# A DLRM tower on one core: the reshaping of the field rows issued from ScalarE, layer 1's items placed later in a step

## What is computed

```python
e = jnp.stack([tbl_f[ids[:, f]] for f in range(24)], axis=1)    # (1024, 24, 16)
X0, Xk, outs = e, e, []
for W in (W0, W1, W2):                                          # 64 outputs each
    Wr = W.reshape(24, Xk.shape[1], 64)
    Xk = jnp.einsum('bfd,bhd,fho->bod', X0, Xk, Wr)
    outs.append(Xk.sum(axis=2))
z = jnp.concatenate(outs, axis=1)
h = jnp.concatenate([z, dense_ctx], axis=1)
h = jnp.maximum(h @ W_top1 + b_top1, 0.0)
h = jnp.maximum(h @ W_top2 + b_top2, 0.0)
y = h @ W_top3
```

## Time and profile before

| | |
|---|---|
| median of 3 runs | 455.85 us (454.94 to 456.58) |
| the profiled execution | 455.96 us, its span 454.1 us |
| TensorE busy | 373.9 us (82%) |
| VectorE busy | 303.0 us (67%) |
| ScalarE busy | 127.6 us (28%) |
| GpSimd busy | 196.5 us (43%) |
| DMA | 64.76 MB, 143 GB/s in the mean |
| mean granted TensorE clock | 0.962 |

### The profile page before, as it was taken

One profiled execution on the slowest core, in us unless ns is written; L12 is line 12 of the kernel. 1 busy time (PEld: TensorE's weight loads), 2 busy tenths in 40 slices (PEclk: granted clock), 3 DMA queues, 4 the chain that ended last, 5 costly groups with the idle time before them and its releaser, 6 DMA issues. The chain is left out here.

```text
span 454.1 us, 6457 instructions
## 1 busy us (share of the span) xinstructions
PE 373.9 (82%) x2436; PEld 140.1 (31%) x2436; DVE 303.0 (67%) x305; ACT 127.6 (28%) x228; POOL 196.5 (43%) x196
## 2 busy tenths in 40 slices
PE   0005957995699899889998998899899998999997
PEld 0002201221134134312441243234333421443554
DVE  1003439887657995899599949994999498991000
ACT  1003000331222333234233333233414241127433
POOL 5777777787777877877707760000000000000000
PEclk9999975996889999999999999999989999999999
DMA  7000088366776787678766776876587558700000
GB/s 205 7 7 7 8 203 199 89 180 173 177 169 184 194 199 172 175 196 201 182 183 184 190 184 193 204 186 190 157 204 190 160 154 208 187 2 0 1 0 0
DMA packets 27203, 64.76 MB, mean 143 GB/s; under 512 B 7247, under 2 KB 10759, under 8 KB 27180
## 3 DMA queue, kind: packets, MB, share of 16 engines
q1 hardware_dynamic: 21036, 62.87, 51.4%
q0 software_dynamic: 6144, 1.59, 3.8%
HBM read 58.06 MB, written 6.38 MB: 142 GB/s over the span
## 5 line engine op out<-in xcount | busy, mean ns | idle before, releaser
L395 DVE TENSOR_TENSOR pairs<-spread,units 128x1024 f32<-128x1024 f32 x192 | 223.3, 1220 | 20.3 <-DMA units<-x_dram 13.1
L367 POOL DMA_INDIRECT emb<-in_tbl,ids_sb x192 | 196.3, 1023 | 74.2 <-issue 57.6
L593 PE MATMUL acc<-pairs,w_sb 128*64 128x512 f32 x768 | 200.3, 624 | 15.7 <-DVE pairs L395 14.6
L395 DVE TENSOR_TENSOR pairs<-turned,common 120x1024 f32<-120x1024 f32 x42 | 51.2, 1220 | 40.9 <-DMA turned<-x_dram 34.4
L593 PEld LDWEIGHTS acc<-pairs,w_sb 128*64 128x64 f32 x768 | 45.4, 139 | 106.9 <-DVE pairs L395 52.9
L593 PE MATMUL acc<-pairs,w 120*64 120x512 f32 x180 | 52.3, 666 | 9.9 <-DVE z L400 5.9
L567 PE MATMUL spread<-x0parts,sel 72*128 72x512 bf16 (+1 forms) x140 | 47.2, 426 | 11.2 <-DVE pairs L395 9.1
L455 ACT ACTIVATE x<-acc 128x512 f32<-128x512 f32 x31 | 18.6, 599 | 117.4 <-PE acc L593 117.4
L610 PE MATMUL misc<-ident_b,parts 128*72 128x128 bf16 x120 | 10.4, 235 | 39.9 <-DVE parts L297 37.0
L468 ACT ACTIVATE x0diag<-misc,mask 128x384 f32<-128x384 f32 x64 | 31.7, 611 | 15.2 <-PE misc L613 15.2
L628 PEld LDWEIGHTS misc<-x0diag,x2t 128*64 128x64 f32 x512 | 26.0, 137 | 18.8 <-issue 16.5
(11 more groups left out here) (38 smaller groups left out, 143.5 us busy)
## 6 DMA issues: line engine op xcount, KB each, us to landing
units<-x_dram SPq DMA_DIRECT2D x64, 512.0 KB, 7.5
turned<-x_dram SPq DMA_DIRECT2D x42, 480.0 KB
x_dram<-x SPq DMA_DIRECT2D x32, 128.0 KB
emb<-in_tbl,ids_sb POOLq DMA_INDIRECT x192
x_dram<-common SPq DMA_DIRECT2D x14, 96.0 KB
x_dram<-common SPq DMA_DIRECT2D x14, 56.0 KB
w_sb<-in_w SPq DMA_DIRECT2D x2, 384.0 KB
wt_sb<-in_wt SPq DMA_DIRECT2D x1, 512.0 KB, 5.5
```

Of the source, the lines that this page charges most:

```text
L367: pool.indirect_dma_start(out=e3[:, f, :], out_offset=None, in_=tables[f], in_offset=bass.IndirectOffsetOnAxis(ap=ids_sb[:, t, f:f + 1], a ...
L395: dve.tensor_tensor(pairs[buf][0:rows, :], source[0:rows, :], other[0:rows, h * HALF:(h + 1) * HALF], ALU.mult).then_inc(pairs_done, 1)
L593: last = pe.matmul(acc[half * H:(half + 1) * H, :], w, pairs[buf][0:rows, half * BLK:(half + 1) * BLK], start=first, stop=final)
```

## The change

ScalarE now issues the stores of common's rows and the loads of turned. `store_fields` follows each `take_common` at once. The three loads for h = 0 are issued at places 7, 8 and 8 of ScalarE's loop (three and four behind the first common), those for h = 1 two places behind the L1 item of h = 0 that frees the buffer. SyncE keeps only the reshaping of x1. In the middle steps and in step 6 the L1 items move from places 12, 14, 16, 21, 23, 26 to 14, 16, 18, 22, 24, 26; step 0 keeps its places. The copy of x1's first half moves with its last item from place 19 to 21.

```diff
+L1_AT = (14, 16, 18, 22, 24, 26)
-MIDDLE = Plan((12, 14, 16, 21, 23, 26), (4, 8), (0, 1), SIDE, {20: 2})
+MIDDLE = Plan(L1_AT, (4, 8), (0, 1), SIDE, {20: 2})
...
-BEFORE_LAST = Plan((12, 14, 16, 21, 23, 26), (4, 8), (0, 1), SIDE)
+BEFORE_LAST = Plan(L1_AT, (4, 8), (0, 1), SIDE)
...
             for t in range(1, TILES):
-                for h in range(2):
-                    turn_fields(t, h)
                 for h in range(2):
                     spread_units(t, t % 2, h)
...
+            def store_fields(i, h):
+
+                act.wait_ge(common_done, 2 * (i + 1) + h + 1)
+                for first, rows in ((0, F), (F, X0_ROWS - F)):
+                    act.dma_start(x0_dram[h][first:first + rows, :],
+                                  common[0:rows * J_CHUNK:J_CHUNK, h * HALF:(h + 1) * HALF]).then_inc(x0_stored[h], 16)
+
+            def turn_fields(i, h, c):
+
+                if c == 0:
+                    act.wait_ge(x0_stored[h], 32 * (i + 1))
+
+                if h == 1:
+                    act.wait_ge(pairs_done, item(i, plan(i).items.index(("L1", c, 0, 0))) + 1)
+                elif has_last(i):
+                    act.wait_ge(pairs_done, item(i - 1, MIDDLE.items.index(("L1", c, 0, 1))) + 1)
+                rows = x0_dram[h][c * J_CHUNK:c * J_CHUNK + F, :].rearrange("f (j x) -> f j x", j=1)
+                strides = [list(d) for d in rows.ap]
+                strides[1] = [HALF, J_CHUNK]
+                act.dma_start(turned[c][:, :], bass.AP(rows.tensor, rows.offset, strides)).then_inc(turned_in[c], 16)
...
                             if n == plan(i).common_at[h]:
                                 use = ("common", h)
                                 take_common(spread_number(i, use), spread_slot(i, use), h)
+                                store_fields(i, h)
+                        for c in range(L1_CHUNKS):
+                            if n == plan(i).common_at[0] + 3 + (c > 0):
+                                turn_fields(i, 0, c)
+                            if n == plan(i).items.index(("L1", c, 0, 0)) + 2:
+                                turn_fields(i, 1, c)
```

More of the change, by code:

```diff
@@ L211, in build_tower @@
         common_done = sem("common_done")
-        x0_stored = sem("x0_stored")
+        x0_stored = [sem(f"x0_stored{h}") for h in range(2)]
         turned_in = [sem(f"turned_in{c}") for c in range(L1_CHUNKS)]
@@ L326, in spread_units @@
                         .then_inc(units_in[slot][h][j], 16)
[L328 to L344, removed]
             for h in range(2):
```

## The result

The changed kernel takes 512.9 us (median; 512.65 to 514.57), the kernel before beside it 456.2. The ratio is 1.124, with a 95% interval from 1.119 to 1.130. It is slower, as forecast, but by 57 us where 14 were forecast, far outside the range. The ratios in this document are taken over fast executions alone and need not be the quotient of the medians beside them, which are over all executions.

What follows compares the result with a forecast made beforehand. A closed loop round each step, 44.0 us, was taken as the bound; the new step was 28.05 + 1.5 + 3.0 + 13.7 = 46.2 us. The last tile's units loads came 14.3 us later: 455.96 + 14.3 = 470.3 us, range 456 to 482.

Steps and rivals of the forecast that it cites:

- The loop: Once round a middle step: common's first copy, x1's copy, x1's stores, units loads, next common; 44.0 us before.
- 461.3 in the sum: Rival that ScalarE's issues cost nothing: a step of 44.7 us, 461.3 in all; chance 0.17.
- x1 behind x0diag, and 17.4 us of pure TensorE work: At place 21 x1's copy waits for 17.4 us of TensorE work, then 3.96 us of x0diag copies on ScalarE.
- x1's stores, 3.0 us: With the turned loads out of their queue, x1's stores take 3.0 us instead of 6.4.
- The units leg, 13.7: From issuing the units loads to the next copy of common: 13.7 us, unchanged.
- An issue on ScalarE, 0.78 us: Each DMA issue on ScalarE costs 0.78 us, the median of a load issue on SyncE.
- the added wait: ScalarE's wait at place 7 for common's stores, landing 4.8 us after the first copy: cost zero.
- common's stores come late: Rival: stores take 9.7 us, the second copy 5.4 us late in six steps, above 500 us; 0.10 shared with clock.
- The four issues: Four issues at place 8 between common's second copy and the first gram copy: 1.5 us of TensorE stalls a step.
- The clock: Rival: TensorE's clock falls after its wait at place 4, some 3 us a step, 485 us; 0.10 shared with late stores.
- 29.55 forecast from common to the end of x1: From common's first copy to the end of x1's copy: 28.05 us plus 1.5 us of stalls.
- faster with 0.14: Rival that units loads stop being a bound, the leg 10.7 us: 451 or 442 us, say 447; chance 0.14.

Runs made afterwards that it cites:

- e2b: The kernel before with only layer 1's items moved to places 14, 16, 18, 22, 24, 26, SyncE issuing everything: 468.9 us, ratio 1.028.
- e4b: The changed kernel with the three loads of turned for h = 0 at places 9, 10, 11 in the middle steps: 469.3 us, ratio 1.029.
- e3b: The changed kernel with ScalarE copying x1's first half ahead of x0diag at place 21 of the middle steps: 494.3 us, ratio 1.084.
- e7: The kernel before with only x1's stores issued by ScalarE, right behind its copy: 459.7 us, ratio 0.996.
- e1b: The changed kernel with layer 1's items back at places 12, 14, 16, 21, 23, 26: 484.8 us, ratio 1.063.
- e6: The kernel before, old places, with ScalarE issuing only common's stores and SyncE keeping the loads of turned: 446.2 us against 458.4, ratio 0.978.
- e9: The changed kernel with 24 useless matmuls ahead of TensorE's wait for gram at place 11: 634.1 us, the kernel before taking 581.2 beside it.
- e5: The changed kernel with useless matmuls ahead of TensorE's waits in the middle steps, 10 at place 4 and 14 at place 11: 510.5 us, ratio 1.119.

## Why the prediction was right or wrong

**The loop** was right: a step is closed by common's first copy, x1's copy, its stores and the units loads, and removing the wait for turned didn't shorten it. In e2b and e4b, which have x1 in its late place without ScalarE's delay, the whole took 468.9 and 469.3 us. That this is close to the 470.3 forecast is luck: they lack the 1.5 us of issues (461.3 in the sum) and have instead the fall of the clock at place 4, 8.3 - 6.1 = 2.2 us a step in e2b.

**x1 behind x0diag, and 17.4 us of pure TensorE work** were right: 17.4 and 17.5 us in e2b and e4b, and e3b gave the order's share, 3 us a step.

**x1's stores, 3.0 us**: measured 2.9 (3.1 in the mean). **The units leg, 13.7**: measured 13.9. **An issue on ScalarE, 0.78 us**: 0.76 to 0.81. Each size held. Of the two reasons given for x1's stores, that the turned loads have landed by then is the one that bears it (the last is issued 7.8 us ahead of them); the other queue is not: e2b has 3.3 us with one queue, e7 5.4 to 7.3 with two.

**The step that failed first is the added wait, taken at zero.** The text put the stores' landing at 4.8 us behind common's copy, from the 3.7 us they take alone. Beside the loads of units they took 8.4 to 8.9 us in the steps 1 to 6, little better than the 8.1 to 9.9 in one queue. Common's second copy came 10.6 us after the first and not 6.1; 4.5 us a step. The Trainium skill (DMA: Bandwidth & Descriptors, Queues, rings and completion order) has a DMA engine serve its queue rows in turn, and by that the stores would have been nearly free. The trace does not agree: for 6.1 us behind the stores' issue q10 moved nothing while q1 had the engines to itself. Whether the engines left q10 waiting or its packets were late in coming to them, the trace doesn't show. The rival "common's stores come late" had the mechanism, was priced at 9.7 us, and shared a chance of 0.10 with the clock, which was too small.

**The four issues** were sized 1.5 us; TensorE's second gram round starts 247.61 - 242.47 = 5.1 us behind common's second copy where it was 177.13 - 173.96 = 3.2. That is 2.0 in this step and 1.9 in the mean.

**The clock** was a rival at place 4 alone. It fell there in the steps 1 to 5 and again at the wait for gram in all six; that wait the sum had at 1.5 us, and it became 3.6 to 5.8. The second fall costs 2.7 us in the mean; in the sum it was zero. The first fall and the wait for the stores run side by side: with the stores' wait and no fall common 1 to 2 is 10.3 to 11.1 us (e1b), with the fall and no such wait 8.3 (e2b), with both 10.6. So stores that landed in time would have given back 2.3 of the 4.5 us, and the clock would have kept the other 2.2.

Together: 29.55 forecast from common to the end of x1, plus 4.5 of stores, 0.4 of issues and 2.7 of clock, is 37.15; measured 37.1. A step is 54.0 us instead of 46.2. x1's stores for the last tile are issued at 430.12 and take 2.9 us, so its loads of units are issued at 433.0 instead of 388.4, 44.6 us later; the profiled execution, 514.6 us, is 44.3 above the forecast. The three terms are not independent: the stores' wait lengthened TensorE's, and that brought the clock down. e4b takes all three away at once, for 43.6 us.

**The chances**: slower had 0.77, rightly. The range was too short above, since the sum had none of these three costs in full and each was at most a rival alone. It also left out more than the text says: faster with 0.14 and clock or late stores with 0.10, priced at 485 and above 500, are 0.24, not under 0.2.

## What to carry to other kernels

In this kernel, a load that had to wait for the landing of a store stood in the program of the engine that copies results out of PSUM. Everything behind it waited too, and TensorE with it, since it had one bank for all side rounds. The stores, which follow that engine's own copy, could be given to it without a loss (e6); the loads that wait for their landing are better left to an engine that has nothing else to do. Price a small store beside large loads at what it costs behind them until a trace shows otherwise, even when it has a queue of its own. Where a new wait falls on TensorE, add the slow stretch after it to the price, but only if nothing else is waited for longer in the same stretch.

## What the runs showed of the hardware that was not expected

- A second hardware queue didn't bring small stores past large loads. In the changed kernel nothing of the two stores (0.16 MB) moved for 6.0 to 6.3 us, until the units loads (2 MB) on the other queue were nearly through; the dependent load came 8.4 to 8.9 us behind the issue, against 8.1 to 9.9 in one queue and 3.7 alone. x1's stores took 5.4 to 7.3 us beside loads of turned (e7), 2.9 with none issued for 7.8 us.
- After TensorE's waits of 2.3 and 3.6 us the granted clock fell to 0.50 (1.2 GHz) for 6.8 us each. With 24 added matmuls up to the end of the second wait it stayed at 1.00 (e9), and in e5 it stayed at 1.00 in the step in which 1.9 us of that wait were left idle. The wait alone doesn't settle it: behind 3.1 us at place 4 of the changed kernel's step 6 the clock did not fall.
- The same program took 456 us in some batches and 580 us in others, with waits of up to 36 us in the latter that the trace ascribes to nothing on the core, and only while gathers were being issued. The cause stays open.
